# Waits between the gathers of an edge loop: GpSimd issues 16 gathers in four sets of four

## The reference

```python
src = jnp.concatenate([edge_index[0], loops])
dst = jnp.concatenate([edge_index[1], loops])
e = jax.nn.leaky_relu(a_src[src] + a_dst[dst], negative_slope=0.2)
ee = jnp.exp(e - e_max[dst])
denom = jax.ops.segment_sum(ee, dst, num_segments=M)
alpha = ee / (denom[dst] + 1e-16)
msg = h[src] * alpha[:, :, None]
agg = jax.ops.segment_sum(msg, dst, num_segments=M).reshape(M, HEADS * NUM_EXPERTS) + b_gat
...
hh = jax.nn.gelu(x @ W1[ei] + b1[ei], approximate=False)
out = out + g[..., None] * (hh @ W2[ei] + b2[ei])
```

## Time and profile before

| | |
|---|---|
| time, median of 3 runs | 4389.0 us (4388.76 to 4391.81) |
| span of the profiled execution | 6367.0 us |
| POOL busy | 2952.7 us (46%) |
| DVE busy | 2796.8 us (44%) |
| PE busy | 4215.6 us (66%) |
| ACT busy | 1151.9 us (18%) |
| gathers of the edge loop | 2180 |

### The profile page before, as it was taken

The page is one execution under the profiler, slowest core; times in us unless marked ns, Lnnn a source line. Parts: engine busy times, 40 slices in busy tenths (PEclk is TensorE's granted clock), DMA queues, the critical chain, the costliest instruction groups (busy, mean ns, idle before and its releaser), DMA issues. The chain is left out here.

```text
span 6367.0 us, 61456 instructions
## 1 busy us (share of the span) xinstructions
PE 4215.6 (66%) x18988; PEld 2885.1 (45%) x19024; DVE 2796.8 (44%) x3513; ACT 1151.9 (18%) x2917; POOL 2952.7 (46%) x2936
## 2 busy tenths in 40 slices
PE   5863357754667777777777767767677777767625
PEld 2543245533445445445445445445445445445500
DVE  8789987753223223223223223223223223233487
ACT  0100000002222222222222222222222222222110
POOL 2008876556444444444444444444444444444328
PEclk7885578765676666666666666666666666676755
DMA  1331157766111111111111111111111111112149
GB/s 46 82 85 44 46 72 100 99 96 54 19 21 22 19 21 21 19 22 21 18 22 21 18 22 21 18 22 21 18 22 21 18 22 21 18 22 20 6 150 355
DMA packets 357674, 284.60 MB, mean 45 GB/s; under 512 B 253586, under 2 KB 329938, under 8 KB 357204
## 3 DMA queue, kind: packets, MB, share of 16 engines
q1 hardware_dynamic: 245620, 199.65, 14.9%
q0 software_dynamic: 87552, 29.20, 5.9%
q10 hardware_dynamic: 24416, 54.71, 3.9%
HBM read 161.06 MB, written 122.27 MB: 44 GB/s over the span
## 5 line engine op out<-in xcount | busy, mean ns | idle before, releaser
L1098 POOL DMA_INDIRECT gath<-tab_d,src_no x2116 | 2001.3, 946 | 2485.8 <-DVE C L1397 1880.9
L1417 DVE TENSOR_TENSOR acc<-acc,C 128x160 f32 x1090 | 349.8, 321 | 2483.8 <-remote 1512.7
L1264 PE MATMUL A<-hid,w2s 128*64 128x392 f32 x1024 | 548.5, 623 | 1210.8 <-ACT hid L1131 1093.1
L1245 PEld LDWEIGHTS C<-spread,lo_hot 128*128 128x128 f32 x4360 | 1106.9, 322 | 335.7 <-issue 311.2
L1245 PE MATMUL C<-spread,lo_hot 128*128 128x160 f32 x4360 | 1180.8, 461 | 50.7 <-issue 27.7
L470 POOL DMA_INDIRECT edge_d<-run_slots,slots x544 | 656.9, 1208 | 683.5 <-ACT run_slots L669 522.3
L1264 PEld LDWEIGHTS A<-hid,w2s 128*64 128x64 f32 x1024 | 111.9, 154 | 1306.9 <-ACT hid L1131 1129.4
L1254 PE MATMUL A<-T,w1s 64*128 64x392 f32 x1024 | 688.9, 765 | 21.8 <-DMA T<-t_d 21.8
L1140 ACT ACTIVATE mlp<-A,b2s 64x392 f32<-64x392 f32 x512 | 298.5, 583 | 2102.9 <-remote 1233.5
L1229 PEld LDWEIGHTS C<-dst_rows,lo_hot_t 128*128 128x128 f32 x4384 | 601.2, 220 | 92.3 <-issue 79.8
L1229 PE MATMUL C<-dst_rows,lo_hot_t 128*128 128x32 f32 x4384 | 619.4, 300 | 12.5 <-ACT lo_hot_t L1126 11.3
(11 more groups left out here) (273 smaller groups left out, 3229.6 us busy)
## 6 DMA issues: line engine op xcount, KB each, us to landing
mlp_d<-mlp ACTq DMA_DIRECT2D x128, 392.0 KB
mlp<-mlp_d SPq DMA_DIRECT2D x64, 784.0 KB, 6.7
gath<-tab_d,src_no POOLq DMA_INDIRECT x2116
pixels<-in_x SPq DMA_DIRECT2D x32, 392.0 KB, 6.5
src<-in_x SPq DMA_DIRECT2D x32, 392.0 KB, 6.5
T<-t_d SPq DMA_DIRECT2D x128, 98.0 KB
X<-x_d SPq DMA_DIRECT2D x64, 196.0 KB, 8.6
out<-X SPq DMA_DIRECT2D x128, 98.0 KB, 7.3
```

What stands on the lines that cost most here:

```text
L1098: pool.indirect_dma_start(gath[:, g % BUFS, j, :], None, node_d if g < BUFS else tab_d, bass.IndirectOffsetOnAxis(ap=src_no[:, t:t + 1], a ...
L1245: mm = pe.matmul(C[:, bank, at:at + HI * VALS], lo_hot[:, k % UNROLL, u * U + j, :], spread[:, u * U + j].rearrange("p h v -> p (h v)"), s ...
L1264: pe.matmul(A[h * CH:(h + 1) * CH, 3, 0:CHUNK], w2s[:, e, :], hid[:], start=True, stop=True).then_inc(s["expert_done"], 1)
L1417: L(dve.tensor_tensor(here, here, C[:, bank, at:at + HI * VALS].rearrange("p (h v) -> p h v", h=HI), ALU.add))
```

## The change

POOL's loop over the tiles of a group gets a wait ahead of tiles 4, 8 and 12, in all groups from the fifth on:

```diff
                     for j in range(G if g < NG - 1 else LAST_TILES):
                         t = g * G + j
+                        if g >= BUFS and j and j % 4 == 0:
+                            pool.wait_ge(gathered[g % BUFS], (g // BUFS * G + j) * 16)
                         pool.indirect_dma_start(gath[:, g % BUFS, j, :], None, node_d if g < BUFS else tab_d,
                                                 bass.IndirectOffsetOnAxis(ap=src_no[:, t:t + 1], axis=0)).then_inc(gathered[g % BUFS], 16)
```

## The result

The changed kernel takes 4954.02 us (median of 3 runs, 4954.02 to 4965.63), against 4389.0: 1.1296 times as long, 95% interval 1.1278 to 1.1315. That is 565 us more. The profiled execution of the changed kernel is itself a run of 4954.02 us, with a span of 4952.3.

What follows compares the result with a forecast made beforehand. The prediction took POOL's issuing of gathers to bound the kernel: 396 waits x 1.10 us = 436 us, plus 35 us for stores, sum 471 us; 4389 + 471 = 4860 us, range 4500 to 5070.

Steps and rivals of the forecast that it cites:

- 8 to 11%: Sign: if the trace shows the waits but time has not grown this much, POOL was not the bound in the runs.
- POOL's issuing bounds the runs: In the edge loop, POOL issues a gather every 1.25 us, 20.0 us a group, and this limits the runs.
- the late signals: DVE's waits for TensorE's signals in the first profile's edge loop, 15.6 us a group, taken as absent from the runs.
- The runs leave 1.217 us a gather: Median 4389.0 us less 1735.9 us outside the edge loop gives 2653 us, spread over 2180 gathers.
- 2.32 us from start to start: At each wait on POOL, next gather starts 2.05 us (landing) plus 0.27 us (reaction) after the one before; adds 1.10 us.
- I take 2.05 for the semaphore: A gather's semaphore was assumed raised 2.05 us after its start, with its last bytes there at 2.0 us.
- The store's term, 35 us: ACT's 128 stores of the MLP's result delay a set's last gather: 128 x 0.3 x 0.9 us.
- The Trainium skill's rule on DVE holding GpSimd off its port: GpSimd cannot write gather descriptors while DVE holds the shared port; as a rival 5480 us, chance 0.03.
- Slack in POOL: Rival: POOL's recorded gap is partly the profile's, so waits are partly hidden; 4389 to 4860 us, middle 4625, chance 0.12.
- Faster: Rival: draining the queue every four gathers lets TensorE's signals through; 4257 us at best, say 4320, chance 0.08.
- TensorE's granted clock: Rival: longer groups keep TensorE's clock at 0.69, so TensorE becomes the bound at 24.5 us a group; 5050 us, chance 0.06.
- The chain without late signals: Work over TensorE, ACT and DVE per group, less DVE's waits for TensorE's signals: 34.1 - 15.6 = 18.5 us.

Runs made afterwards that it cites:

- seven_waits: The changed kernel with seven waits a group (eight sets of two gathers, 924 waits) instead of three: 5739.52 us, ratio 1.3074 to the kernel before.
- twelve_sets: Kernel before, but only 12 of 16 gathers a group from the fifth group on, in three sets of four with two waits (264 waits): 4301.44 us, ratio 0.9775.
- twelve: Kernel before, without added waits, but from the fifth group on only 12 of the 16 gathers a group are issued: 4305.07 us, ratio 0.9783.

## Why the prediction was right, point by point

The forecast was slower, 4860 us; it is 4954, inside the range from 4500 to 5070 but above the 4800 to 4930 that the forecast gave itself. The loss is 565 instead of 471 us, 13% where 8 to 11% was named as the sign. The mechanism is the one forecast: 396 waits, each ended by a landing, on the queue that bounds the kernel.

*POOL's issuing bounds the runs.* Right. The prediction read it out of a trace in which POOL waits 14 us a group, from the argument that the runs have no room for the late signals. It took those signals for a mark of the profiled execution; they were the mark of one execution, and the span of 6838 us that it gave for the changed kernel under the profiler came out as 4952.3. The second profile of the kernel before shows the bound directly: gathers 1.250 us apart throughout, and no late signals. The three wait counts and the nearly proportional loss show it independently. What the prediction did not see is how close TensorE is: it sets the pace of DVE's groups in the first part of the loop, and POOL is the bound by 0.66 us a group.

*The runs leave 1.217 us a gather.* A little off. It is 1.250 us, as POOL's own rows said; the time outside the loop, taken from the odd execution, was 108 us too long.

*2.32 us from start to start.* This term was mis-sized, and nearly alone makes the difference. Measured are 0.944 + 1.742 = 2.69 us in the mean. The bytes were timed right (1.9 to 2.0 us after the start), and so was the reaction. Off was the step "I take 2.05 for the semaphore": the landing comes 2.4 us after the start in the trace of `seven_waits`. In the trace of the changed kernel the last recorded update of the gather's semaphore ahead of POOL's 396 waits comes 2.37 us after the start (median), and POOL starts its next gather 0.26 us after that update each time, close to the 0.27 us of the earlier trace rows. So the delay lies in the landing and not in the waiting engine: some 0.5 us pass between the last byte and the semaphore. A wait then adds 1.742 - 0.305 (662.1 over 2173 gaps) = 1.437 us, and 396 of them 569 us, where 565 was measured.

*The store's term, 35 us.* Too large for this kernel. Of the 396 waits 28 are longer than 1.9 us, by 26 us in all over the median of 1.68 us. 20 of these 28 end behind 4425 us, when the last store (issued at 4417.58) is past; the bytes of one such gather, started at 4543.95, move until 2.9 us after its start, and why was not tried. The other 8 make 7 us, and the longest of them meets a store:

```profile
1460.55 0.94 POOL L1100 DMA_INDIRECT gath<-tab_d,src_no  x1 [0.30 <-issue]
1460.66 0.48 ACTq L1146 DMA_DIRECT2D mlp_d<-mlp  x1
1464.93 0.94 POOL L1100 DMA_INDIRECT gath<-tab_d,src_no  x1 [3.43 <-DMA gath<-tab_d,src_no]
```

So the effect is real, but the term took the store to fall anywhere in a group, with a chance of 0.3 to hit. It depends on how the sets lie against the store instead: with the same bounds as in `twelve_sets`, 3 waits meet one of the 128 stores here, and 80 there. That the sum came within 94 us is in part luck: the 35 us made up for some of the 110 us by which the waits alone were too cheap (436 against 396 x (1.684 - 0.305) = 546).

*The Trainium skill's rule on DVE holding GpSimd off its port* ("SBUF — State Buffer", the box on DVE blocking a DMA issued from GpSimd, which ties it to a DVE operation in a two-port mode) was weighed at nothing in the sum and at 0.03 as a rival. In the loop nothing of it is seen: 2116 gathers of the changed kernel take between 938 and 961 ns. The Trainium skill's rule to issue early and wait late ("DMA: Bandwidth & Descriptors", Rules for kernel authors) is borne out where the issuing engine binds, at 1.43 us a wait; `twelve_sets` shows its other side, that an engine with time to spare can wait early for free.

*The rivals.* Slack in POOL: there is none in the full kernel, since one wait a group is already paid in full; it appears only once POOL issues a quarter less. Faster: the late signals on which it rested are not in the second profile of the kernel before, so there was nothing to relieve. TensorE's granted clock did fall with the longer groups, from 0.89 to 0.81 in the stretch from 1600 to 3600 us, and to 0.74 with seven waits, but TensorE was also less busy there (1672.32 and 1342.81 of 2000 us) and did not take over as the bound. The chain without late signals was taken at 18.5 us; the next bound is at 19.1, and it is TensorE.

What remains open is why the one execution of 6367 us was so slow inside the loop. No other showed it, and no run was made to bring it about.

## What to carry to other kernels

Compare the span of a profile with the time of the runs first; where they differ, take rates of single instructions from it, and not who waits for whom. An engine that issues small transfers back to back can be the bound at 76% busy: the fixed gap between its instructions counts. A wait for a landing on such an engine costs the whole way from the transfer's start to the next instruction, less the engine's own pace, every time; on an engine with room it costs nothing. Which of the two holds can be tried by issuing a few transfers less. A second engine at 98% may then be found close behind.

## What the runs showed of the hardware that wasn't expected

A gather of 128 rows of 96 bytes has its bytes in place 1.9 us after its start, but its semaphore is complete only at 2.4 us, and an instruction that waits for it starts at 2.6 to 2.7 us. The wait itself, when met, costs less than 0.3% of the kernel for 396 of them. A store of 392 KB that is issued at the same time as a gather lengthened the wait for that gather from 1.7 to as much as 3.4 us. And the kernel before has two engines almost level: POOL at 20.0 us a group, and TensorE at 19.1 by the rows of `twelve`, with 17.3 us where its granted clock is 1.00 and 20.6 where it is 0.83.
